# Sixteen unread float32 products of 32 rows in place of fifteen unread transposes at the start of TensorE's program

## What is computed

```
xn = _layernorm(x)
qkv = xn @ w_attn + b_attn                      # 16 heads of 8
scores = einsum(q, k) * 8 ** -0.5 + (-log(distance + 1)), -inf above the diagonal
attn = softmax(scores);  out = (attn @ v) @ w_proj + b_proj
gate, up = fp4(xn) @ fp4(w_gate).T, fp4(xn) @ fp4(w_up).T
h = silu(gate) * up
return x + out + fp4(h) @ fp4(w_down).T
```

## Time and profile before

| | us |
|---|---|
| median of 3 runs (626.72 to 627.9) | 627.3 |
| the profiled execution, its own time | 626.35 |
| its span, first to last instruction | 624.5 |
| PE busy, share of the span | 564.4, 90% |
| DVE busy | 562.8, 90% |
| POOL busy | 537.4, 86% |
| ACT busy | 400.8, 64% |

### The profile page before, as it was taken

How to read it: one execution, slowest core, us unless ns; L and a number is a source line. 1 busy time by engine, 2 the same in 40 slices (tenths; PEclk the granted TensorE clock), 3 DMA queues, 4 the chain that set the end, 5 groups by cost and what they waited for, 6 DMA issues and landing times.

```text
span 624.5 us, 11270 instructions
## 1 busy us (share of the span) xinstructions
PE 564.4 (90%) x3807; PEld 250.9 (40%) x3807; DVE 562.8 (90%) x1178; ACT 400.8 (64%) x857; POOL 537.4 (86%) x400
## 2 busy tenths in 40 slices
PE   6999779999999999999989899999989898989985
PEld 5576534444343334333333332342334242432322
DVE  6899998989999999999999999998989999997661
ACT  4576457566656475767667577666656667759782
POOL 7226987789899989999998999999998999998992
PEclk9999988999999999999999999999999999999997
DMA  5255341310000000200000000000000000000000
GB/s 148 74 137 114 119 83 51 78 43 36 2 2 3 0 2 10 86 1 2 2 0 2 19 1 1 2 2 1 1 2 1 19 0 2 1 2 1 1 2 17
DMA packets 14715, 16.66 MB, mean 27 GB/s; under 512 B 1594, under 2 KB 14171, under 8 KB 14243
## 3 DMA queue, kind: packets, MB, share of 16 engines
q1 hardware_dynamic: 14123, 15.70, 9.2%
q10 hardware_dynamic: 536, 0.26, 0.2%
HBM read 11.75 MB, written 4.01 MB: 25 GB/s over the span
## 4 chain that ended last, share of the span: by engine, by line
PE 43%; POOL 32%; DVE 13%; ACT 7%; issue 4%; ACTq 0%; POOLq 0%; DVEq 0%
POOL ring L802 25%; PE psum L1396 11%; PE psum L1354 9%; PE psum L1378 7%; DVE mxp L1135 7%; ACT ring L954 2%; POOL xw L820 2%; POOL xw L818 2%; PE psum L1331 2%; POOL xw L822 2%; PE psum L1312 2%; PE psum L1314 1%; PE psum L1320 1%; DVE ring L1162 1%; PE psum L1404 1%
## 5 line engine op out<-in xcount | busy, mean ns | idle before, releaser
L802 POOL TENSOR_TENSOR ring<-ring,dist 128x1024 f32<-128x1024 f32 (+3 forms) x223 | 438.4, 1996 | 31.7 <-ACT ring L954 31.3
L1135 DVE TENSOR_REDUCE mxp<-psum 128x1 f32<-128x512 f32 (+3 forms) x640 | 352.6, 598 | 20.5 <-PE psum L1354 11.4
L954 ACT ACTIVATE ring<-psum 128x512 f32<-128x512 f32 (+3 forms) x446 | 211.5, 528 | 101.5 <-PE psum L1381 51.9
L1354 PE MATMUL psum<-kop,qop 96*128 96x512 bf16 (+3 forms) x640 | 198.0, 352 | 7.3 <-DVE mxp L1135 5.3
L1378 PE MATMUL psum<-qop,kop 128*128 128x512 bf16 (+3 forms) x640 | 190.7, 349 | 6.2 <-DVE mxp L1135 3.7
L1396 PE MATMUL psum<-ring,vaug 128*32 128x512 f32 (+3 forms) x1280 | 151.5, 544 | 15.0 <-POOL ring L802 14.1
L1162 DVE TENSOR_TENSOR ring<-psum,dist 128x512 f32<-128x512 f32 (+3 forms) x194 | 115.7, 622 | 13.9 <-ACT psum L954 13.8
L954 ACT ACTIVATE psum<-psum 128x512 f32<-128x512 f32 (+3 forms) x194 | 99.5, 543 | 39.7 <-PE psum L1378 23.4
L1354 PEld LDWEIGHTS psum<-kop,qop 96*128 96x128 bf16 x640 | 57.2, 97 | 127.8 <-DVE mxp L1135 46.5
L1378 PEld LDWEIGHTS psum<-qop,kop 128*128 128x128 bf16 x640 | 59.7, 97 | 82.2 <-DVE mxp L1135 15.5
L1357 PE MATMUL psum<-tri_q,identb 128*128 128x128 bf16 x256 | 56.2, 221 | 0.0
(11 more groups left out here) (130 smaller groups left out, 490.2 us busy)
## 6 DMA issues: line engine op xcount, KB each, us to landing
kop<-parts_dram SPq DMA_DIRECT2D x9, 384.0 KB
qop<-parts_dram SPq DMA_DIRECT2D x9, 384.0 KB
parts_dram<-qpart SPq DMA_DIRECT2D x18, 128.0 KB, 2.8
xin<-_attn_hidden_states_dram SPq DMA_DIRECT2D x4, 256.0 KB, 4.7
ring<-inv_dram SPq DMA_DIRECT2D x1, 1024.0 KB, 4.9
out_dram<-xin SPq DMA_DIRECT2D x4, 256.0 KB, 2.3
parts_dram<-qpart SPq DMA_DIRECT2D x6, 96.0 KB
qop<-parts_dram SPq DMA_DIRECT2D x3, 192.0 KB
```

What stands on the lines that cost most here:

```text
L802: g_.tensor_tensor(slot(p)[:, :, 0:n], slot(p)[:, :, 0:n], both, ALU.mult).then_inc(weighed_pool, 1)
L954: a_.activation(scores if pair_vec[p] else slot(p)[:, e % 2, 0:n], scores, ACT.Exp, scale=SCALE).then_inc(exp_done, 1)
L1135: v_.tensor_reduce(mxp[:, u % 2, 4 * a + j, c - g:c - g + 1], bank(*o)[:, 0:n], AX_X, ALU.max).then_inc(max_used, 1)
L1354: ins = mm(bank(*o)[:, 0:n], qop[0:K_MAX, u // NQ % 2, h, P * a:P * (a + 1)], kop[0:K_MAX, h, k0:k0 + n], start=True, stop=(c != g))
```

## The change

PE's opening block is edited and nothing else. Fifteen of the 30 transposes stay. In place of the others come four rounds (`ROW_WARM`). A round is four float32 products, each with 32 rows of `identf` (rows 32j to 32j + 31) as the stationary operand and the same 32 rows, repeated four times to 512 columns, as the moving one. The operands of the four lie in four different row groups of the array, and the results, 128 partitions by 512 columns each, go to four different PSUM banks (0 to 3). After the second and the fourth round come four bfloat16 products of the whole 128x128 array (`identb` by itself), added to the first 128 columns of the same banks. None of the results is read. No wait and no signal is added or removed.

```
-            for _ in range(WARM):
+            for _ in range(WARM // 2):
                 nc.tensor.transpose(psum[:, OUT_BANK, 0:P], identf[:], identf[:])
+            wide = identf[:].rearrange("p (o n) -> p o n", o=1).to_broadcast([P, 4, P])
+            for k in range(ROW_WARM):
+                for j in range(4):
+                    rows = slice(32 * j, 32 * j + 32)
+                    mm(psum[:, j, :], identf[rows, :], wide[rows], start=True, stop=k % 2 == 0)
+                if k % 2:
+                    for j in range(4):
+                        mm(psum[:, j, 0:P], identb[:], identb[:], start=False, stop=True)
```

More of the change, by code:

```diff
@@ L42 @@
 WARM = 30
+ROW_WARM = 4
 NEG = -1e30
```

## The result

The changed kernel takes 629.35 us (median of 5 runs, 628.7 to 629.96) against 626.75 us for the kernel before in the runs beside it (median of 5). The two medians differ by 2.6 us. The ratio with its 95% interval is 1.0034 (1.0022 to 1.0045), that is +2.1 us (1.4 to 2.8); it is not the quotient of the two medians (1.0041). The profiled execution took 628.7 us with a span of 627.0; before it was 626.35 and 624.5.

A forecast was written before the change was run, and what follows sets the result against it. No engine bounds the whole chain; PE's uncovered opening block delays everything after L1250. Added 4.44 us minus 1.64 us saved gives +2.8 us, passed through whole: 627.3 + 2.8 = 630.1 us, range 628.0 to 635.0 us.

The forecast's parts named there:

- The path: PE's opening block before L1250: unread work already 2.5 us too long, nothing covers it, so additions delay the start of everything.
- The removed transposes: PE's opening block: the 15 transposes removed are fast ones, 15 x 0.109 = 1.64 us saved.
- The rounds: Added products in PE's opening block: four row groups run side by side, 2.22 us a pair of rounds, 4.44 us for two.
- The passing on: From L1250 to the end: the whole 2.8 us delay passes through, with no pool of idle time to cover it.
- faster: Rival, PE's slow clock stretches after two short gaps: full speed gives back 4.0 us, net -1.2 us, 626.1 us; chance 0.07.
- The point: Whole kernel: forecast median of 630.1 us, from 627.3 + 2.8, 0.45% slower.
- Serial products: Rival, added rounds: row groups do not run side by side, +13.5 us, 640.8 us; chance 0.10.
- The half-way case: Rival, added rounds: products overlap only by halves, 4 us more, about 634.3 us; chance 0.08.
- The clock did not fall behind the rounds: Rival, PE during or behind the rounds: 32-row products count as little work, clock falls to 1.2 GHz, 631.8 to 633.5 us; chance 0.06.
- The rule of the Trainium skill on transposes: Rival, PE's opening: transposes do not raise the clock, products do; 0.7 us less before L1260; chance 0.01.

The follow-up runs named there:

- trans55: The kernel before with 55 unread opening transposes instead of 30 and no row groups: 629.75 us, ratio 1.0036.
- rows8: The changed kernel with 8 rounds of row-group products instead of 4: 634.36 us, ratio 1.0104 to the kernel before.
- half15: The kernel before with 15 instead of 30 unread opening transposes and nothing in their place: 624.68 us against 627.8, ratio 0.9957.
- nofill: The kernel before without the 21 fillers between the opening transposes and L1250: 624.37 us, ratio 0.9950.
- bf16rows: The changed kernel with bfloat16 instead of float32 row-group products and 16 rounds instead of 4: 632.01 us, one run.
- again: The changed kernel unchanged, measured once more beside two shorter openings: 629.99 us, ratio 1.0038 to the kernel before.
- nobetween: The changed kernel without the eight whole-array products, four rounds in one piece: 628.15 us against 625.96 for the kernel before, one run.
- after_nofill: The changed kernel without the first 21 fillers ahead of its first wanted transposes: 627.82 us, ratio 1.0008 to the kernel before.
- the control: The run wholearray: the changed kernel with its 16 float32 products on all 128 rows, 639.13 us against 626.03 for the kernel before.
- onegroup: The changed kernel with all 16 float32 products on rows 0 to 31, one row group: 654.91 us against 625.96 for the kernel before, one run.
- mixed: The changed kernel with each row-group product of the second and fourth round followed at once by its whole-array product: 640.15 us, one run.
- wholearray: The changed kernel with all 16 float32 products on all 128 rows: 639.13 us against 626.03 for the kernel before, one run.

## Why the prediction was right, step by step

**The path.** That nothing covers PE's opening block was the base of it. It holds in both directions: more work (trans55, rows8) and less (half15, nofill) moved L1250 and everything behind it by their own price.

**The removed transposes.** 15 x 0.109 = 1.64 us; half15 shows D = -1.67.

**The rounds.** The price was taken from column groups, 0.10 for the entry, 0.90, 1.00 and 0.22: 2.22 us a pair. It is 2.26. The way in and out costs 0.32 us of it (2.26 - 2 x 0.86 - 0.22) and not 0.2; the rounds between, 0.86 us instead of 0.90 and more, make up for most of that. The weight loads of 128 columns, 184 ns each here instead of the 140 of the earlier trace rows, hide all the same. Net +2.77 us at L1259, +2.8 predicted. The Trainium skill (TensorE: Matmul & The Clock Gate, Part 3, measured speedup) gives four row groups a factor of 3.07, without naming a type; by that, an estimate, L1259 would have come 0.7 us later. The runs show 3.44/0.86 = 4.0 in float32, between rounds that follow each other. In bfloat16 they show 3.1 with the way in and out counted. Whether the skill's factor counts them too, no run here shows.

**The passing on.** "I pass the whole 2.8 us through" holds to two hundredths up to 220 us in the changed kernel, and in all traces of the table between 40 and 66 us. Two things lie on top. Between 66 and 118 us the shift moves by S = -0.78 to +0.81 us, from kernel to kernel and for the changed kernel itself (+0.02 and -0.66); the clock's slow stretches lie elsewhere in each execution, and their length there differs too (6.8 us in half15, 13.7 in bf16rows, 10.2 in the others), so it is what they happen to hit that differs. The rival "faster" named this mechanism and put it at 4 us; the runs show it at under 1 us, and as scatter, not as a gain. And from 230 us to the end every trace loses 0.1 to 0.3 us against that of the kernel before, the slower-made and the faster-made ones alike; that points to something in that one trace, and I don't know its cause. Near the end (from 616.2 us on in the kernel before) the clock is at half once more in every trace; in again and nobetween the shift grows there by another 0.4 to 0.5 us.

**The time.** The point was 630.1 us, measured 629.35 and, in the second set, 629.99. Part of the miss is the start: the point rests on 627.3 us for the kernel before, which had a median of 626.75 beside the changed one. The change is +2.1 and +2.4 us by the ratios (2.6 and 2.3 by the medians), a little under 2.8. The short versions gain more than their D by 0.5 to 1.0 us, the long ones lose 0.4 to 0.8 us less, and after_nofill alone agrees. It looks as if the kernel before had by 0.5 us more of the clock's scatter in its median than the others. That wasn't tested; what is shown is the traces' D.

**The rivals.** Serial products did not come, and the control prices them: +13.1 us, where the prediction had 13.5. It would have been more on one row group, where the clock stayed low. (The half-way case was given as 634.3 us; its own terms, 630.1 + 4, make 634.1.) The clock did not fall behind the rounds, a case that was given 0.06. But a low clock beside products of 32 rows is real: it stayed low through those of onegroup and fell behind those of mixed, where one row group worked at a time (in mixed, in half of the rounds). In the changed kernel, with all four at work side by side, it stayed up, and in rows8 it rose among such rounds. The rule of the Trainium skill on transposes (same page, Part 4, PE-mode transpose), that they don't bring the full clock, is refused again: in trans55 the clock rose at 10.10 us, when nothing but transposes had run.

## What to carry to other kernels

Work that nobody reads is free only while the engine would wait anyway: put its end beside the moment when the first wanted input is ready (here 10.18 us), and drop what is beyond. Before comparing two traces, align them by when the clock rose; here that alone moved the same program by up to 1.5 us. A product on a part of TensorE's rows is as cheap as its neighbours make it: four products on four row groups in a row cost as much as one, on one row group they cost four, and there the clock stayed low (onegroup) or fell (mixed).

## What was not expected of the hardware

TensorE stayed at 1.2 GHz for 35 us, from 5.68 to 40.8 us, while it was busy without a gap, with float32 products on one row group for most of that time. Serial products on all rows, begun when it had just risen to 2.4 GHz (8.71 us), left it there, and so did four row groups side by side. Changing from the whole array to row groups and back costs 0.2 to 0.3 us together in float32 (0.32 a pair in the changed kernel, 0.30 in mixed, 0.18 between transposes in nobetween). And a float32 weight load of 32 rows by 128 columns took 184 ns in the changed kernel, hardly less than the 190 ns of 128 by 128 in wholearray.
